# A transformer stack on one core: the router's ranks computed by distance between experts, the loop of the grouped attention written out, and the query and key terms stored batch by batch

## The reference, cut to what matters

```
logits = xf @ router_w.T
scores = jax.nn.sigmoid(logits)
sb = scores + correction_bias
grp_top = jax.lax.top_k(sb.reshape(S, G, EPG), PER_GROUP_K)[0]
group_scores = grp_top.sum(axis=-1)
_, group_idx = jax.lax.top_k(group_scores, TOPK_GROUP)
...
masked = jnp.where(score_mask > 0, sb, -jnp.inf)
_, topk_idx = jax.lax.top_k(masked, K)
w = jnp.take_along_axis(scores, topk_idx, axis=1)
w = w / (w.sum(axis=-1, keepdims=True) + 1e-20)
```

## Time and profile before

| | |
|---|---|
| runs | 5901.5 us median of 3 (5891.1 to 5905.9) |
| the profiled execution | 5919.2 us, its span 5917.5 us |
| mean granted clock of PE | 0.881 |
| PE, DVE, ACT, POOL busy | 76%, 65%, 49%, 34% of the span |
| `a0` and `t0` | from 18.0 to 165.4 us and from 169.5 to 852.1 us |
| `t1`, `t3`, `t7` | from 1538.5 to 1976.5, 4876.1 to 5299.7, 5526.3 to 5845.9 us |
| `r3` | from 2063.2 to 2161.9 us |

### The profile page before, as it was taken

The page is one execution under the profiler, slowest core; times in us unless marked ns, Lnnn a source line. Parts: engine busy times, 40 slices in busy tenths (PEclk is TensorE's granted clock), DMA queues, the critical chain, the costliest instruction groups (busy, mean ns, idle before and its releaser), DMA issues. The chain is left out here.

```text
span 5917.5 us, 94345 instructions
## 1 busy us (share of the span) xinstructions
PE 4496.5 (76%) x24994; PEld 2859.1 (48%) x24994; DVE 3860.9 (65%) x8228; ACT 2892.7 (49%) x6091; POOL 2017.6 (34%) x3169
## 2 busy tenths in 40 slices
PE   7677774657799639985758676987677978977897
PEld 3344343545333328852336455865555843335434
DVE  6566665684588654435779675579665557885466
ACT  2566652351377422225546565345665325763353
POOL 0344420000566202214435541245541216531342
PEclk9798987879799769987779898999899988997797
DMA  6999960001533211116523321013320054333443
GB/s 224 299 309 312 313 214 17 0 0 66 175 91 93 50 54 43 42 41 150 145 65 121 120 70 32 8 67 126 101 68 26 6 183 101 98 72 113 144 119 102
DMA packets 327011, 648.06 MB, mean 110 GB/s; under 512 B 73202, under 2 KB 140435, under 8 KB 326632
## 3 DMA queue, kind: packets, MB, share of 16 engines
q1 hardware_dynamic: 259544, 463.30, 24.1%
q0 software_dynamic: 67104, 180.70, 11.0%
HBM read 361.41 MB, written 251.28 MB: 104 GB/s over the span
## 5 line engine op out<-in xcount | busy, mean ns | idle before, releaser
L828 DVE TENSOR_REDUCE t_nmax<-t_aps 128x2 f32<-128x1024 f32 x700 | 837.8, 1221 | 271.6 <-PE t_aps L750 265.8
L935 ACT ACTIVATE t_expT<-t_bps 128x512 f32<-128x512 f32 x1290 | 700.7, 599 | 278.2 <-PE t_bps L769 233.2
L769 PE MATMUL t_bps<-t_Q,t_K 51*128 51x512 f32 (+2 forms) x1290 | 524.0, 468 | 56.4 <-ACT t_expT L935 39.8
L750 PE MATMUL t_aps<-t_K,t_Q 49*128 49x512 f32 (+2 forms) x1400 | 463.4, 459 | 64.3 <-DMA t_K<-k_halves 28.0
L769 PEld LDWEIGHTS t_bps<-t_Q,t_K 51*128 51x128 f32 (+2 forms) x1290 | 228.1, 189 | 522.5 <-ACT t_expT L935 369.6
L2173 DVE TENSOR_TENSOR f_hl<-f_h,f_hh 128x512 fp32r<-128x512 f32 x192 | 203.3, 1059 | 410.8 <-ACT f_hh L2098 410.8
L796 PE MATMUL t_ops<-t_expT,t_V 128*17 128x512 f32 (+1 forms) x2560 | 413.5, 613 | 0.4 <-ACT t_expT L935 0.4
L3610 ACT ACTIVATE t_relsb<-t_relsb,t_nmax 128x128 f32<-128x128 f32 (+3 forms) x512 | 288.7, 564 | 219.9 <-DVE t_nmax L3582 219.2
L3488 POOL TENSOR_TENSOR t_relsb<-t_relsb,t_M 128x128 f32<-128x128 f32 x512 | 216.7, 454 | 387.9 <-DMA t_relsb<-rel 387.8
L2465 POOL TENSOR_TENSOR a_crossed<-a_qsb,a_tab 128x256 f32<-128x256 f32 x272 | 262.3, 985 | 250.4 <-ACT a_qsb L2412 217.5
L3241 ACT ACTIVATE t_prob<-t_summed,t_nmax,norms 128x256 f32<-128x256 f32 (+1 forms) x560 | 317.3, 571 | 33.8 <-DVE t_nmax L3300 33.7
(11 more groups left out here) (456 smaller groups left out, 12444.7 us busy)
## 6 DMA issues: line engine op xcount, KB each, us to landing
rel<-t_rows SPq DMA_DIRECT2D x128, 640.0 KB, 4.9
t_relsb<-rel SPq DMA_DIRECT2D x128, 640.0 KB, 6.6
t_Q<-q_halves POOLq DMA_DIRECT2D x420, 64.0 KB, 2.5
t_K<-k_halves POOLq DMA_DIRECT2D x420, 64.0 KB, 2.6
k_halves<-a_parts SPq DMA_DIRECT2D x48, 512.0 KB, 4.9
q_halves<-a_parts SPq DMA_DIRECT2D x48, 512.0 KB, 5.4
o_xT<-attended SPq DMA_DIRECT2D x32, 512.0 KB, 4.0
f_R<-combine SPq DMA_DIRECT2D x128, 128.0 KB, 3.1
```

The source lines that it names most:

```text
L750: last = nc.tensor.matmul(aps[:, (t * PPG + i) % 2, x, :], operand(Qr, KA, p, h, slice(t * P, (t + 1) * P)), operand(Kr, KA, p, h, slice(0 ...
L769: nc.tensor.matmul(bps[:, slot_of(kb, j), :], operand(Kr, KB, p, h, slice(kb * P, (kb + 1) * P)), operand(Qr, KB, p, h, slice(0, S)), star ...
L828: nc.vector.tensor_reduce(nmax[:, g, t, i * HPT:(i + 1) * HPT], aps[:, (t * PPG + i) % 2], AX.X, ALU.max, negate=True).then_inc(s["maxed"], 1)
L935: nc.scalar.activation(expT[:, kb % RING, j, :], bps[:, slot_of(kb, j), :], ACT.Exp).then_inc(s["expo"], 1 + (PAD if end else 0))
```

## The change

Three edits. In `route` the logits come out with the tokens on partitions (the tile of tokens is the stationary operand, the router's 16 columns move), so neither copy nor turning precedes the sigmoid. Tokens are worked in two halves. A rank is made by distance: for each distance d the experts e and e+d are compared once each way, greater-or-equal for the later one and greater for the earlier one, which settles ties without the table; the results go into a zeroed square and one reduction sums it. In `grouped_attention` the hardware loop of `steps` becomes a Python loop. `q_terms` and `k_terms` get the shape [NB, 6, D, S]; the load of four heads then finds each partition's 4 x 512 numbers in one piece of DRAM.

```diff
@@ qkv, grouped_attention
-                            sp.dma_start(dst.rearrange("r f t -> f r t")[row:row + P, first:first + many, ds(b * S, S)], terms).then_inc(s[f"parts_st{j}"], 16)
+                            sp.dma_start(dst[ds(b, 1), first:first + many, row:row + P, :].rearrange("o r f t -> f (o r) t"), terms).then_inc(s[f"parts_st{j}"], 16)
@@ def steps(eng, step):
-                with eng.Fori(0, NB // 2) as it:
+                for it in range(NB // 2):
@@ route
+    NP = 2
+    PT = TT // NP
+            @block.gpsimd
+            def _(pool):
+                nc.gpsimd.memset(first[:, :, :, :], 0.0).then_inc(s["zero"], 1)
+                nc.gpsimd.memset(ahead[:, 0:PT, :, :], 0.0).then_inc(s["zero"], 1)
+                nc.gpsimd.memset(ahead[:, PT:TT, :, :], 0.0).then_inc(s["zero"], 1)
...
+                for q in range(NP):
+                    for t in range(PT):
                         for k in range(KT):
-                            last = nc.tensor.matmul(lps[0:E, p, :], RW[:, k, :], xT[:, k, ds(b * S, S)], start=k == 0, stop=k == KT - 1)
+                            last = nc.tensor.matmul(lps[:, q, t * E:(t + 1) * E], xT[:, k, (q * PT + t) * P:(q * PT + t + 1) * P], RW[:, k, :],
+                                                    start=k == 0, stop=k == KT - 1)
+                    last.then_inc(s["lg"], 1)
...
+                for q in range(NP):
+                    act.wait_ge(s["lg"], q + 1)
+                    nc.scalar.activation(score[:, q * PT:(q + 1) * PT, :].rearrange("p t e -> p (t e)"), lps[:, q, 0:PT * E], ACT.Sigmoid).then_inc(s["sc"], 1)
...
-                def rank(x, n, out, limit):
+                def rank(x, n, room, out, limit):
...
-                    V.tensor_tensor(gv, other, one, ALU.is_gt)
-                    ch.link(V.tensor_tensor(ev, other, one, ALU.is_equal))
-                    ch.link(V.tensor_tensor(ev, ev, before[:, 0:n, 0:n].unsqueeze(1).broadcast_to([P, T, n, n]), ALU.mult))
-                    ch.link(V.tensor_tensor(gv, gv, ev, ALU.add))
-                    ch.link(V.tensor_reduce(out, gv, AX.X, ALU.add))
+                    for d in range(1, n):
+                        below = bass.AP(corner.tensor, corner.offset + d * n, [rows, [n * n, T], [n + 1, n - d]])
+                        above = bass.AP(corner.tensor, corner.offset + d, [rows, [n * n, T], [n + 1, n - d]])
+                        V.tensor_tensor(below, x[:, :, 0:n - d], x[:, :, d:n], ALU.is_ge)
+                        last = V.tensor_tensor(above, x[:, :, d:n], x[:, :, 0:n - d], ALU.is_gt)
+                    ch.link(last)
+                    ch.link(V.tensor_reduce(out, room, AX.X, ALU.add))
                     ch.link(V.tensor_scalar(out, out, float(limit) - 0.5, None, ALU.is_lt))
@@ relative_attention, program
-                        pool.dma_start(dst[:, p, h:h + H // QH, :], src.rearrange("r (d h) t -> (r d) h t", h=H)[:, h:h + H // QH, b * S:(b + 1) * S]).then_inc(s[f"{what}{p}"], 16)
+                        pool.dma_start(dst[:, p, h:h + H // QH, :], src[b].rearrange("r (d h) t -> (r d) h t", h=H)[:, h:h + H // QH, :]).then_inc(s[f"{what}{p}"], 16)
-        qs = dram("q_terms", [6, D, TOK], BF16)
-        ks = dram("k_terms", [6, D, TOK], BF16)
+        qs = dram("q_terms", [NB, 6, D, S], BF16)
+        ks = dram("k_terms", [NB, 6, D, S], BF16)
```

More of the change, by code:

```diff
@@ L1676, in route @@
     E, GR, EPG, TOPG, TOPK = 16, 4, 4, 2, 4
-    QT = TT // 4
-    with phase(nc, name, "w lg lg_cp lt sc comb ct ct_cp out dvc") as (s, sb, ps):
+    NP = 2
+    PT = TT // NP
+    with phase(nc, name, "w lg sc zero comb ct ct_cp out dvc") as (s, sb, ps):
         combT = sb("combT", [E, TOK])
@@ L1681, in route @@
         cb = sb("cb", [P, E])
-        before = sb("before", [P, E, E])
-        lg = sb("lg", [E, 2, S])
         score = sb("score", [P, TT, E])
@@ L1690, in route @@
         g2 = sb("g2", [P, TT, GR])
-        gt = sb("gt", [P, QT, E, E])
-        eq = sb("eq", [P, QT, E, E])
+        ahead = sb("ahead", [P, TT, E, E])
+        first = sb("first", [P, TT, GR, GR])
         tot = sb("tot", [P, TT])
-        lps = ps("lps", [P, 2, S])
-        tps = ps("tps", [P, 2, S])
-        cps = ps("cps", [P, 2, S])
+        lps = ps("lps", [P, NP, S])
+        cps = ps("cps", [P, 4, S])
         with nc.Block() as block:
@@ L1702, in _ @@
                 sp.dma_start(cb[:, :], bias.unsqueeze(0).broadcast_to([P, E])).then_inc(s["w"], 16)
[L1703 to L1706 removed]
+                for q in range(NP):
+                    part = slice(q * PT * P, (q + 1) * PT * P)
+                    sp.wait_ge(s["ct_cp"], (q + 1) * NB // NP)
+                    sp.dma_start(comb_rows[:, part], combT[:, part]).then_inc(s["out"], 16)
@@ L1708, in _ @@
+                sp.wait_ge(s["out"], 16 * NP)
+            @block.gpsimd
[3 more added lines that the diff above has]
+                nc.gpsimd.memset(ahead[:, PT:TT, :, :], 0.0).then_inc(s["zero"], 1)
             @block.tensor
             def _(pe):
-                pe.wait_ge(s["w"], 48)
-                with pe.Fori(0, NB // 2) as it:
-                    for p in range(2):
-                        b = it * 2 + p
-                        pe.wait_ge(s["lg_cp"], b + 1)
-                        for k in range(KT):
-                            last = nc.tensor.matmul(lps[0:E, p, :], RW[:, k, :], xT[:, k, ds(b * S, S)], start=k == 0, stop=k == KT - 1)
-                        last.then_inc(s["lg"], 1)
-                        pe.wait_ge(s["lg_cp"], b + 3)
-                        pe.wait_ge(s["sc"], b + 1)
-                        alone(pe)
-                        for t in range(NT):
-                            last = nc.tensor.transpose(tps[:, p, t * E:(t + 1) * E], lg[:, p, t * P:(t + 1) * P], G.ident[0:E, 0:E])
-                        last.then_inc(s["lt"], 1)
@@ L1752, in _ @@
                 V = nc.vector
-                dve.wait_ge(s["w"], 48)
-                dve.wait_ge(s["sc"], NB + 2)
-                ch.link(V.tensor_tensor(biased[:, :, :], score[:, :, :], cb[:, :].unsqueeze(1).broadcast_to([P, TT, E]), ALU.add))
-                bg = biased[:, :, :].rearrange("p t (g i) -> p (t g) i", i=EPG)
-                h, l = (x[:, :, :, :].rearrange("p t g i -> p (t g) i") for x in (hi, lo))
-                g, r = (x[:, :, :].rearrange("p t g -> p (t g)").unsqueeze(2) for x in (gs, g2))
@@ L1780, in _ @@
-                rank(gs[:, :, :], GR, g2[:, :, :], TOPG)
-                each = g2[:, :, :].rearrange("p t g -> p (t g)").unsqueeze(2).broadcast_to([P, TT * GR, EPG])
-                ch.link(V.tensor_tensor(bg, bg, each, ALU.mult))
-                ch.link(V.tensor_scalar(g2[:, :, :], g2[:, :, :], 1.0, BIG, ALU.subtract, ALU.mult))
-                ch.link(V.tensor_tensor(bg, bg, each, ALU.add))
-                for q in range(4):
-                    rank(biased[:, q * QT:(q + 1) * QT, :], E, comb[:, q * QT:(q + 1) * QT, :], TOPK)
@@ new lines, in _ @@
+                dve.wait_ge(s["w"], 32)
+                for q in range(NP):
+                    part = slice(q * PT, (q + 1) * PT)
+                    dve.wait_ge(s["sc"], q + 1)
+                    ch.link(V.tensor_tensor(biased[:, part, :], score[:, part, :], cb[:, :].unsqueeze(1).broadcast_to([P, PT, E]), ALU.add))
+                    bg = biased[:, part, :].rearrange("p t (g i) -> p (t g) i", i=EPG)
+                    h, l = (x[:, part, :, :].rearrange("p t g i -> p (t g) i") for x in (hi, lo))
+                    g, r = (x[:, part, :].rearrange("p t g -> p (t g)").unsqueeze(2) for x in (gs, g2))
+                    V.tensor_tensor(h, bg[:, :, 0:2], bg[:, :, 2:4], ALU.max)
+                    ch.link(V.tensor_tensor(l, bg[:, :, 0:2], bg[:, :, 2:4], ALU.min))
+                    V.tensor_tensor(g, h[:, :, 0:1], h[:, :, 1:2], ALU.max)
+                    ch.link(V.tensor_tensor(r, h[:, :, 0:1], h[:, :, 1:2], ALU.min))
+                    ch.link(V.tensor_tensor(h[:, :, 0:1], l[:, :, 0:1], l[:, :, 1:2], ALU.max))
+                    ch.link(V.tensor_tensor(r, r, h[:, :, 0:1], ALU.max))
+                    ch.link(V.tensor_tensor(gs[:, part, :], gs[:, part, :], g2[:, part, :], ALU.add))
+                    dve.wait_ge(s["zero"], q + 2)
+                    rank(gs[:, part, :], GR, first[:, part], g2[:, part, :], TOPG)
+                    each = g2[:, part, :].rearrange("p t g -> p (t g)").unsqueeze(2).broadcast_to([P, PT * GR, EPG])
+                    ch.link(V.tensor_tensor(bg, bg, each, ALU.mult))
+                    ch.link(V.tensor_scalar(g2[:, part, :], g2[:, part, :], 1.0, BIG, ALU.subtract, ALU.mult))
+                    ch.link(V.tensor_tensor(bg, bg, each, ALU.add))
+                    rank(biased[:, part, :], E, ahead[:, part], comb[:, part, :], TOPK)
+                    ch.link(V.tensor_tensor(comb[:, part, :], comb[:, part, :], score[:, part, :], ALU.mult))
+                    ch.link(V.tensor_reduce(tot[:, part], comb[:, part, :], AX.X, ALU.add))
```

(3 more changed lines are left out.)

41 lines of the change are left out of this document (9 added, 32 removed).

## The result

| | before | after |
|---|---|---|
| runs beside each other | 5897.7 us, median of 5 (5888.8 to 5905.9) | 5859.5 us, median of 5 (5844.4 to 5867.5) |
| ratio | | 0.9938, 95% interval 0.9924 to 0.9951 |
| profiled execution | 5919.2 us | 5867.5 us |
| `r3`, up to the first instruction of the next phase | 103.1 us | 62.0 us |
| `t1`, `t3`, `t7` | 438.0, 423.7, 319.6 us | 429.0, 422.0, 320.0 us |

The change saves 0.6%, some 37 us (29 to 45 by the interval), where 58 were forecast. Between the two profiled executions it is 52 us, and these lie in few places: 41 in and behind `r3`, 9 in `t1`, 2 in `t3`, nothing in `t0` or `t7`. Elsewhere shifts of some us cancel, the largest 6 us less in `cell` and 6 more in the two of `windowed_attention`, whose code is the same; these two kinds of phase differ by 9 to 12 us among the profiles of all runs.

The account below looks back on a forecast made before the run. It took `r3` as bound by three parts end to end, `t1` by DVE's maxima and a PE-ACT chain, `t0` by PE's clock. Gains of 41.3 + 8 + 5 + 4 = 58.3 us gave 5843 us, own range 5826 to 5859.

Parts of the forecast that it names:

- rival (a): Whole kernel: only the route pays, a loop behind `t1` stalls, short operations cost full price; 5869 us, chance 0.13.
- Route, front: In `r3` before DVE starts: logits from 16-column passes let DVE start earlier; gain 16.5 us, bounds 14.0 and 28.
- Route, choice: In `r3`, DVE's work alone: two halves take 36.2 us against 58.5; gain 22.3 us.
- Route, end: In `r3` after DVE: four batches instead of eight remain to be turned and stored; gain 2.5 us.
- Attention, turns of the loop: In `t1`: three loop turns lose 2.7 us each; gain 8 us, bounds 0 and 9; nothing in `t3` and `t7`.
- Attention, registers: In `t1` and `t3`: ACT's lost register operations count behind the copy of shifts; gain 5 us, bounds 0 and 29.
- Terms, loads: At the start of `t0`: Q and K load faster, so PE waits less; gain 4 us, bounds 0 and 7.
- the step on later loads: In `t0`: later loads save some 3 us of queue time a batch, which nothing waits for; 0, at most 10.
- Terms, stores: Stores of the terms: still one run of 512 numbers a partition and row, hidden under DVE's splitting; 0 us.
- (c): In the three written-out loop bodies: straight code stalls its engines, making the kernel slower; 6235 us, chance 0.03.
- (b): Whole kernel: the chain of PE and ACT gains more, with weight loads faster than with 128 columns; 5820 us, chance 0.12.
- (d): In `r3`: the route doesn't get shorter, as short strided operations run at several times the price; 5900 us, chance 0.02.

## Why the prediction was right, and where not

The direction and the range held; the forecast of 5843 was 16 us below the median of 5859.5. That median lies at the edge of the forecast's own narrower range (5826 to 5859) and is nearer to the 5869 of rival (a); the repeat of the changed kernel took 5853.5. By its steps:

- *Route, front*, 16.5 us: 33.1 - 17.45 = 15.7. The 0.22 us a pass was right (0.215). The clock's rise after 9.2 us of work didn't come, so the last 22 passes of the first half cost 4.7 us instead of 2.4. PE started 3.1 us into the phase instead of 4.5, as the table was no longer waited for, which the step had put at nothing; 1.4 of the 2.3 us cancel.
- *Route, choice*, 22.3 us: 58.5 - 36.9 = 21.6. Up to 128 elements the short operations cost what the step had (0.22 us at 128, 0.09 at 16), above that more: 0.42 at 240 where it had 0.33. By the sign that it gave itself (0.1 us plus the elements) the longest ones are too far apart, and the price of an element was the part that was mis-sized. One that writes 240 elements into the square lasts 0.58 us, the addition of the bias over 256 in a row 0.43; whether the strides do this, no run separates. A whole half takes 18.45 us where the step had 18.1. The Trainium skill, "VectorE: DVE Perf Modes", section on the errata of SBUF sources, would have had 5.5 us less gain, an estimate; the trace has 0.7 less.
- *Route, end*, 2.5 us: measured 7.1 - 4.6 = 2.5. Another 1.3 us, which no step had, lie behind it: from the issue of the last store to the next phase it is 3.4 instead of 4.7 us, as half of the weights were stored earlier. The route in all: 41.1 against 41.3, or 39.8 by the means of all profiles.
- *Attention, turns of the loop*, 8 us: the step that failed; it gave nothing. `t1` as a whole went from a mean of 434.9 us (seven profiles with the loops kept) to 430.5 (four with ACT written out and POOL's pauses). But its first group's copy comes 62 to 67 us into the phase with either code, so the cleaner measure is from there to the last group's copy: 363.1 to 366.4 us, mean 364.7, against 362.0 to 362.8, mean 362.4. That is 2.3 us, and the pace alone gives 31 x 0.115 = 3.6. The step asked what hides the fetching of straight code and found it rightly harmless, but wrote "POOL and SP keep theirs" without asking what those cost. SP's first two turns show no pause (0.2 to 0.3 us). POOL paused 2.8 to 3.7 us at its two turns in the kernels with the loops kept as well, but there the pause was covered, as POOL's timeline of the kernel before shows:

```profile
1697.32 0.80 POOL L874 DMA_DIRECT2D t_V<-values  x1 [0.22 <-issue]
1703.11 0.20 POOL L881 CAST t_mparts<-t_nmax 128x16 fp32r<-128x16 f32 x1 [4.99 <-DVE t_nmax L828]
```

POOL executed its next instruction at 1700.8, but the maxima that it splits were ready only at 1703.0, in the group that ACT's pause had made late. In 12 of the 14 such turns of the seven profiles the maxima ended behind POOL's return, in the other two 0.1 and 0.3 us ahead of it. Once ACT's pause is gone POOL's stands alone, at a price of 2.7 to 6.0 us. The three runs without either pause have 353.3 us from the first copy to the last, 11.4 less than with the loops, so the step's 8 us were there to be had. Not run, and so only argued from the waits, is the kernel before without POOL's pauses alone.

- *Attention, registers*, 5 us: the size held by luck. The pace fell by 0.115 us a group instead of 0.07, but only a third of it from ACT. That is 3.6 us in `t1`, of which POOL's pauses leave 2.3, and 3.0 in `t3` from the first copy to the last. (In the profiled pair `t3` shows 1.7, as the first copy came at 64.0 instead of 62.6 us; over all profiles that start lies anywhere from 59.7 to 64.0.)
- *Terms, loads*, 4 us: nothing. The start came 1.5 us earlier (forecast 2.1) and the phase did not end earlier: the means of the two layouts differ by 1.3 us, less than two profiles of one kernel do. The pace of `t0` stayed with PE's clock, as the step on later loads had it. *Terms, stores*, 0: `qkv` 147.5 and 147.3 us.

Sum with the sizes measured: 39.8 + 2.3 + 3.0 + 0 = 45 us, where 58.3 were forecast; it lies between the measured 37 (29 to 45) and the repeat's 48 (35 to 62). The 52 us between the two profiled executions contain 3 us of a long `t1` before (438.0 against a mean of 434.9) and 1 of a long `r3`.

Of the rivals, (c) is excluded: no engine stalled in the straight code. (a) named the right thing in the wrong place: a stall did take the place of the one removed, in POOL's loop of the same phase. Its own form, a stall in a loop behind `t1`, is what the route edit does when it is alone, and there costs 13 us in `t3`; the written-out loop covered this up in the whole change. By the phases the two edits are worth 27 and 5 us alone and 45 together. Measured were 24, 37 and 22 us in the three kernels with the route alone and 10 with the loop alone, so the route alone would be taken for less than the 40 us that it takes off its phase. (b) is not borne out: passes of 16 columns run no faster than those of 128 had, 0.215 us, and the clock in `t1` dips still, behind POOL's pause. (d) is excluded by `r3`.

What isn't settled is why ACT's loop in `t3` pauses with the route edit, as the same place in its program doesn't prevent it.

## What to carry to other kernels

When a stall of one engine at a loop's turn is removed, look at the turn of every other engine's loop of that phase: a pause near it can cost nothing as long as the first is there, and its full price afterwards. A pause can be dearer than its length where PE waits with it, as in one of the two groups here PEclk was 0.58 for the work behind. And an edit in one phase can bring up a stall in another that wasn't touched, so each phase's time is compared, not only the changed one's.

## What the runs showed of the hardware

- A pause of 3 us on POOL cost `t1` 2.7 us once and 5.9 us the other time; PEclk was 0.86 over the 12 us behind it in the first case and 0.58 over 15 us in the second. The kernel with the loop alone shows the same pair: 14.6 us at 0.86 and 17.4 at 0.57.
- Behind a loop's taken branch the next instruction came 2.3 to 3.3 us later on ACT and 2.8 to 3.8 on POOL where it stalled, 0.06 to 0.3 us later on the engines and in the loops that showed no stall.
- One phase of unchanged code, with PE busy 83 to 87% of it, took 116, 129 or 144 us, at a mean PEclk of 0.81, 0.72 or 0.63. That is up to 28 us from one execution to the next, close to what the whole change saves.
- 128 passes of 16 columns, each behind a float weight load of 128x128, took 0.215 us each over 27.5 us, with PEclk at 0.50 throughout.
- POOL's two pauses at a loop's turn vanished when its code was moved by 67 instructions, with no other edit: `t1` went from a mean of 430.5 to 423.3 us, and between first and last copy from 362.4 to 353.3. ACT's pauses stayed in a kernel that put `t3`'s loop back to its old place in ACT's program.
